# One kernel, one core: the order of work in the attention rounds changed, with the mask bias moved to VectorE

## What is computed

```python
x = x + xattn(layernorm(x), ctx, ctx, mask, gamma, beta)   # 16 x 64 queries, 1601 keys, keys are also the values
    # logits = q k^T / sqrt(512); where mask == 0: -9e15; softmax; sum over ctx; normalize; * gamma + beta
x = x + attn(layernorm(x), W_qkv, W_out)                   # softmax over the 64 rows of the own sequence
x = x + ffn(layernorm(x), router_w, expert_w1, expert_w2)  # top 2 of 8 experts, gelu, weighed by the softmax of the two
```

## Time and profile before

| what | value |
|---|---|
| median of 3 runs | 754.7 us (754.33 to 756.3) |
| the profiled execution's own time | 754.9 us |
| its span | 753.2 us |
| mean granted PE clock | 0.998 |
| PE busy | 733.2 us (97%) |
| PEld busy | 554.5 us (74%) |
| DVE busy | 435.3 us (58%) |
| ACT busy | 310.1 us (41%) |
| POOL busy | 156.3 us (21%) |
| PE in the chain that ended last | 85% of the span |
| DMA in that chain | 7% |

### The profile page before, as it was taken

How to read it: one execution, slowest core, us unless ns; L and a number is a source line. 1 busy time by engine, 2 the same in 40 slices (tenths; PEclk the granted TensorE clock), 3 DMA queues, 4 the chain that set the end, 5 groups by cost and what they waited for, 6 DMA issues and landing times.

```text
span 753.2 us, 12302 instructions
## 1 busy us (share of the span) xinstructions
PE 733.2 (97%) x4760; PEld 554.5 (74%) x4760; DVE 435.3 (58%) x980; ACT 310.1 (41%) x520; POOL 156.3 (21%) x162
## 2 busy tenths in 40 slices
PE   7899999999999999999999999999999999999996
PEld 5444354545455454578999999999999998888885
DVE  5423456666666663768975455555555565565631
ACT  2122212121212121355555556555565665656631
POOL 2132130505050401123510301310211211120201
PEclk9999999999999999999999999999999999999999
DMA  9999999999999999940645635745665656674602
GB/s 312 402 418 418 396 403 414 407 413 404 418 402 419 401 420 400 371 152 30 208 151 195 168 122 193 199 166 198 174 222 167 214 184 209 234 207 175 175 2 29
DMA packets 36477, 199.40 MB, mean 265 GB/s; under 512 B 4716, under 2 KB 5372, under 8 KB 15680
## 3 DMA queue, kind: packets, MB, share of 16 engines
q1 hardware_dynamic: 29912, 186.74, 64.5%
q0 software_dynamic: 4704, 9.14, 6.4%
q10 hardware_dynamic: 1800, 2.70, 1.1%
HBM read 188.19 MB, written 10.37 MB: 264 GB/s over the span
## 4 chain that ended last, share of the span: by engine, by line
PE 85%; DMA 7%; DVE 3%; SPq 2%; issue 1%; ACT 1%; POOL 0%; POOLq 0%
PE ps L854 11%; PE ps L813 9%; PE ps L1078 8%; PE ps L1080 8%; PE ps L1079 8%; PE ps L1100 4%; PE ps L1101 4%; PE ps L1102 4%; PE ps L1109 4%; PE ps L1110 4%; PE ps L1111 4%; PE ps L869 3%; DMA arena<-in_w_qkv 3%; DMA arena<-in_ctx 3%; PE ps L781 2%; PE ps L788 1%
## 5 line engine op out<-in xcount | busy, mean ns | idle before, releaser
L485 POOL TENSOR_TENSOR small<-small 128x1 f32<-128x1 f32 x64 | 24.4, 381 | 547.8 <-DVE yb_space L1709 196.2
L1080 PE MATMUL ps<-xT,low_a 128*128 128x288 f32 (+5 forms) x384 | 110.2, 287 | 0.0
L1291 ACT ACTIVATE hid<-ps 128x288 f32<-128x288 f32 (+5 forms) x128 | 50.6, 395 | 141.8 <-PE ps L1080 139.4
L1678 DVE TENSOR_TENSOR h_ring<-hid,h_ring 128x288 fp32r<-128x288 f32 (+5 forms) x128 | 55.6, 435 | 83.6 <-ACT h_ring L1296 83.6
L854 PE MATMUL ps<-arena 128*64 128x512 f32 (+1 forms) x416 | 95.4, 599 | 1.6 <-DMA arena<-in_ctx 0.8
L1530 DVE TENSOR_TENSOR low_a<-w_raw_a,high_b 128x2048 fp32r<-128x2048 f32 x32 | 73.3, 2291 | 37.8 <-ACT high_b L1218 37.8
L813 PE MATMUL ps<-arena 128*64 128x512 f32 x384 | 85.9, 596 | 1.1 <-DMA arena<-in_ctx_turned 0.8
L1158 ACT COPY arena<-ps 128x512 f32<-128x512 f32 (+2 forms) x90 | 42.0, 526 | 100.7 <-PE ps L788 62.8
L1078 PE MATMUL ps<-xT,high_b 128*128 128x288 f32 (+5 forms) x256 | 74.9, 293 | 0.0
L1079 PE MATMUL ps<-xT,high_b 128*128 128x288 f32 (+5 forms) x256 | 73.4, 287 | 0.0
L1080 PEld LDWEIGHTS ps<-xT,low_a 128*128 128x128 f32 x384 | 72.5, 189 | 0.0
(11 more groups left out here) (219 smaller groups left out, 1629.9 us busy)
## 6 DMA issues: line engine op xcount, KB each, us to landing
arena<-in_ctx_turned SPq DMA_DIRECT2D x48, 1024.0 KB, 22.8
arena<-in_ctx SPq DMA_DIRECT2D x48, 1024.0 KB, 18.9
w_raw_a<-in_w SPq DMA_DIRECT2D x48, 1024.0 KB, 4.9
w_raw_b<-in_w SPq DMA_DIRECT2D x16, 1024.0 KB, 4.8
arena<-in_mask SPq DMA_DIRECT2D x8, 800.5 KB, 21.4
tokens_x<-arena SPq DMA_DIRECT2D x11, 256.0 KB, 13.1
arena<-in_w_qkv SPq DMA_DIRECT2D x8, 256.0 KB, 4.7
out<-res SPq DMA_DIRECT2D x8, 256.0 KB, 9.2
```

The lines of the kernel that those rows point to most:

```text
L1080: mm = pe.matmul(o, w_low[2 * f][:, cols], high[:, k, 0:w.width], start=False, stop=(k == KC - 1))
L1291: nc.scalar.activation(hid[:, c % 2, 0:w.width], bank(c % UP_BANKS)[:, 0:w.width], ACT.Gelu).then_inc(gelu_done, 1)
L1678: dve.tensor_tensor(h_ring[:, c % RING, 1, 0:w.width], hid[:, c % 2, 0:w.width], h_ring[:, c % RING, 0, 0:w.width].bitcast(F32), ALU.subtr ...
```

## The change

The diff's parts, in the program's order. SP: the first weights for values are loaded before the first mask and the third turned block; x's tiles 3 to 7 come one by one, tile r+2 in round r. The mask bias moves from POOL to DVE (`bounds` in the DVE list: twice around `softmax(0)`, then once a round ahead of `queries`). PE: the three score blocks and the remainder stand together; `turn_second` and the router of tile r-3 come after them; `ranks` comes behind `values`; the three long `sums` stand together and `weigh` behind them. ACT's copies and DVE's routing steps follow that order. In the tail `turn_second(5)` comes ahead of the sums of tile 7 and `router(5)` behind the first of them. `fill_order` is rewritten to match.

```diff
@@ fill_order @@
-        for kind, t in (("logit", r - 3), ("xn", r - 2), ("qr", r), ("rank", r - 3), ("g", r - 2), ("s", r - 2),
-                        ("u", r - 2), ("pt", r - 2), ("out", r - 2), ("xq", r + 1), ("rest0", r + 1),
-                        ("rest1", r + 1), ("xr", r - 2)):
+        for kind, t in (("qr", r), ("xn", r - 2), ("xr", r - 3), ("g", r - 2), ("logit", r - 3), ("s", r - 2),
+                        ("u", r - 2), ("rank", r - 3), ("pt", r - 2), ("out", r - 2), ("xq", r + 1), ("rest0", r + 1),
+                        ("rest1", r + 1)):
...
@@ SP @@
             load_rest(0)
+            load_turned(0, 0)
+            load_turned(0, 1)
+            sp.dma_start(raw_v, ...).then_inc(wv_in, 16)
             load_mask(0)
-            for blk in range(NBLK - 1):
-                load_turned(0, blk)
-            sp.dma_start(raw_v, ...).then_inc(wv_in, 16)
+            load_turned(0, 2)
...
-                if r == 1:
-                    sp.dma_start(res[:, 3 * D:]..., x[3 * P:, :]...).then_inc(x_rest_in, 16)
+                if runs(r + 2):
+                    sp.dma_start(tile_of(r + 2), x[(r + 2) * P:(r + 3) * P, :]).then_inc(x_later_in[r % 2], 16)
@@ POOL: bounds() and its calls go; DVE @@
+            def bounds(j):
+                dve.wait_ge(mask_in, j * 16 + 16)
+                dve.tensor_scalar(bound, mask_sb, 0, MASKED - LIMIT, ALU.is_equal, ALU.mult).then_inc(bound_ready, 1)
@@ PE, in a round @@
                 turn_prob(r - 1)
-                if runs(r - 3):
-                    router(r - 3)
-                scores(r, 0)
-                scores(r, 1)
+                for blk in range(NBLK - 1):
+                    scores(r, blk)
+                rest_scores(r)
                 if runs(r - 2):
                     turn_first(r - 2)
-                scores(r, 2)
-                rest_scores(r)
                 if runs(r - 3):
-                    ranks(r - 3)
+                    turn_second(r - 3)
...
                     keys(r - 2)
+                if runs(r - 3):
+                    router(r - 3)
                 sums(r - 1, PV_ORDER[0])
                 if runs(r - 2):
                     own_scores(r - 2)
                     values(r - 2)
-                sums(r - 1, PV_ORDER[1])
+                if runs(r - 3):
+                    ranks(r - 3)
                 if runs(r - 2):
                     turn_own_probs(r - 2)
+                sums(r - 1, PV_ORDER[1])
                 sums(r - 1, PV_ORDER[2])
+                sums(r - 1, PV_ORDER[3])
                 if runs(r - 2):
                     weigh(r - 2)
-                sums(r - 1, PV_ORDER[3])
                 if runs(r + 1):
                     turn_query(r + 1)
                     turn_rest(r + 1)
-                if runs(r - 2):
-                    turn_second(r - 2)
 
             turn_prob(LAST)
+            turn_second(LAST - 2)
+            sums(LAST, PV_ORDER[0])
             router(LAST - 2)
-            sums(LAST, PV_ORDER[0])
             sums(LAST, PV_ORDER[1])
@@ ACT, in a round @@
+                    copy_fill("xr", r - 3, xrT, shown=by_chunk)
-                    gate_exp(r - 3)
                 exps(r)
                 if runs(r - 2):
                     copy_fill("g", r - 2, gT, shown=by_chunk)
+                if runs(r - 3):
+                    gate_exp(r - 3)
...
-                if runs(r - 2):
-                    copy_fill("xr", r - 2, xrT, shown=by_chunk)
@@ DVE @@
+            bounds(0)
             softmax(0)
+            bounds(1)
...
-                if runs(r - 3):
-                    route_first(r - 3)
-                    route_ratio(r - 3)
                 softmax(r)
                 if runs(r - 2):
                     low_xn(r - 2)
                 if runs(r - 3):
-                    gates(r - 3)
-                    route_rank(r - 3)
-                    route_second(r - 3)
+                    route_first(r - 3)
+                    route_ratio(r - 3)
                 if runs(r - 2):
                     tops(r - 2)
+                if runs(r - 3):
+                    route_rank(r - 3)
+                    gates(r - 3)
+                    route_second(r - 3)
                 if runs(r + 1):
+                    bounds(r + 1)
                     queries(r + 1)
```

More of the change, by code:

```diff
@@ L96, in fill_order @@
         yield "p", LAST, n
-    for kind, t in (("logit", LAST - 2), ("xn", LAST - 1), ("rank", LAST - 2), ("g", LAST - 1), ("s", LAST - 1),
+    for kind, t in (("xr", LAST - 2), ("logit", LAST - 2), ("xn", LAST - 1), ("rank", LAST - 2), ("g", LAST - 1), ("s", LAST - 1),
                     ("u", LAST - 1), ("pt", LAST - 1), ("xn", LAST), ("out", LAST - 1), ("g", LAST),
@@ L400, in bank @@
             return ps[:, i * BLK:(i + n) * BLK]
-        x_in, x1_in, x2_in, x_rest_in = sem("x_in"), sem("x1_in"), sem("x2_in"), sem("x_rest_in")
+        x_in, x1_in, x2_in = sem("x_in"), sem("x1_in"), sem("x2_in")
+        x_later_in = [sem(f"x_later_in{i}") for i in range(2)]
         id_in, cst_in, gb_in = sem("id_in"), sem("cst_in"), sem("gb_in")
@@ L537, in _ @@
             load_rest(0)
+            load_turned(0, 0)
+            load_turned(0, 1)
+            sp.dma_start(raw_v, w_qkv[:, 2 * WBLK:].rearrange("p (k h) -> p k h", k=KC)).then_inc(wv_in, 16)
             load_mask(0)
-            for blk in range(NBLK - 1):
-                load_turned(0, blk)
-            sp.dma_start(raw_v, w_qkv[:, 2 * WBLK:].rearrange("p (k h) -> p k h", k=KC)).then_inc(wv_in, 16)
+            load_turned(0, 2)
             sp.dma_start(raw_out, w_out.rearrange("p (k h) -> p k h", k=KC)).then_inc(wo_in, 16)
@@ L559, in _ @@
                         load_turned(r + 1, blk)
-                if r == 1:
-                    sp.dma_start(res[:, 3 * D:].rearrange("p (t d) -> p t d", d=D),
-                                 x[3 * P:, :].rearrange("(t p) d -> p t d", p=P)).then_inc(x_rest_in, 16)
+                if runs(r + 2):
+                    sp.dma_start(tile_of(r + 2), x[(r + 2) * P:(r + 3) * P, :]).then_inc(x_later_in[r % 2], 16)
                 for blk in range(NBLK - 1):
@@ L617, in _ @@
             own = Steps(pool, p_own)
[L619 to L625, removed]
             def add_bias(j):
@@ L654, in _ @@
                 pool.memset(small[:, 24 + n:25 + n], 0.0).then_inc(places_free, 1)
-            bounds(0)
             pool.wait_ge(gb_in, 32)
             add_bias(0)
-            bounds(1)
             pool.wait_ge(zero_out, 16)
@@ L661, in _ @@
                 add_bias(r)
-                if runs(r + 1):
-                    bounds(r + 1)
                 if runs(r - 3):
@@ L1261, in _ @@
                     copy_rest(r + 1)
-                if runs(r - 2):
-                    copy_fill("xr", r - 2, xrT, shown=by_chunk)
             copy_probs(LAST)
+            copy_fill("xr", LAST - 2, xrT, shown=by_chunk)
             gate_exp(LAST - 2)
@@ L1384, in queries @@
             def queries(p):
-                dve.wait_ge((x_in, x1_in, x2_in, x_rest_in)[min(p, 3)], 16)
+                if p < 3:
+                    dve.wait_ge((x_in, x1_in, x2_in)[p], 16)
+                else:
+                    dve.wait_ge(x_later_in[p % 2], (p - 1) // 2 * 16)
                 if p >= 1:
@@ L1416, in attended @@
                 if j == 0:
+                    dve.wait_ge(gb_in, 32)
                     dve.wait_ge(filled, filled_at("vo", 0, KC - 1))
```

## The result

The changed kernel takes 760.7 us (median of 6 executions, 759.9 to 761.7) beside 755.2 for the kernel before in the same session (753.8 to 756.3): the ratio is 1.0073 [1.0063, 1.0084]. It is slower by 5.5 us, more than the 0.3% that can be told from no change, and it lies above the range of the prediction (753.3 to 759.3). The profiled execution has 760.06 us of its own time and a span of 758.3, 5.1 over the span before. Its mean granted clock of PE is 0.991 (0.998 before).

What follows compares the result with a forecast made beforehand. Loads set the pace up to 114.56 us, PE after that, DVE joining at the end of round 7. -4.2 + 5.0 + 0.9 = +1.7 on 754.9 gave 756.6 profiled, 756.4 us median; range 753.3 to 759.3.

Steps and rivals of the forecast that it cites:

- The step that failed: Tail: from tile 7's first sums PE runs gapless to `keys(6)`, only the router's 0.9 us added, all behind follows.
- the tail's waits: Tail: `weigh(5)` ends last, DVE's 7.5 us follow nearly uncovered; tile 7's sums start 0.85 us later, 5.0 of the gain gone.
- the router: Tail: tile 5's router, formerly done while PE waited for DVE, now stands among tile 7's sums: 0.9 us more.
- The gain ahead of the tail: Up to T (end of `rest_scores`) of round 7: 2.4 us by round 3 plus 4 x 0.45, 4.2 us gained.
- Breaks between 64 and 128 columns: PE, each round: six stretches of 64-column work become three, 0.29 us per break pair, 0.87 us a round saved.
- The two short waits: PE, each round: `keys` waits 0.24 us for ACT's copy, `turn_prob` 0.2 for its banks; together bounded by 0 and 0.8.
- Wait (b): Ahead of `turn_prob`: its banks must be freed by copies of `weigh`'s result and of the query; 0.2 us a round.
- Rival (1): Slower: waits at `keys` and `turn_prob` cost their upper bound, 0.4 us more a round; 758.6 us; chance 0.25.
- rival (2): Waits at `keys` and `turn_prob` cost nothing, 5 x 0.44 us less; 754.4 us; chance 0.15.
- before 92: Sign of being wrong: round 2's third score block starting before 92 us; forecast 92.7, set by its turned context landing.
- Rival (3): Faster: the 1.6 us gained at the start pass through if round 2's turned context lands earlier; up to 752.8; chance 0.12.
- rival (4): DVE late inside rounds: late mask or longer stretch holds the query, `copy_pt` and `weigh`; 761 us; chance 0.03.

Runs made afterwards that it cites:

- experiment 1: Changed kernel plus products nobody reads (20 ahead of tile 5's second turn, 24 ahead of tile 7's first sums); 757.5 us, 1.0031 of the kernel before.
- experiment 6: Kernel of experiment 5 with `weigh` ahead of the last long sums in every round, not only round 7; 755.03 us, 0.9995 of the kernel before.
- experiment 9: Kernel of experiment 5 with the first loads in their old order (values' weights behind mask and third turned block); 753.42 us, 0.9979 of the kernel before.
- experiment 11: Kernel of experiment 10 plus products nobody reads in PE's waits (34 ahead of tile 5's second turn, 7 ahead of tile 7's sums); 758.05 us, 1.0047.
- experiment 10: Kernel before the change with `weigh(5)` moved behind the last long sums, in round 7 alone; 761.14 us, 1.0076 of the kernel before.
- experiment 8: Kernel of experiment 5 with x's tiles 3 to 7 in one load again, in round 1; 755.78 us, 1.0006 of the kernel before.
- experiment 7: Kernel of experiment 5 with the mask bias back on POOL; 754.31 us, 0.9984 of the kernel before.
- kernel 4: Changed kernel with `weigh` ahead of the last sums in round 7 alone and tile 5's router back ahead of tile 7's first sums; 753.98 us, 0.9981.
- kernel 12: Kernel of experiment 5 with 9 more products nobody reads, in short waits before the experts begin; 752.58 us, 0.9965 of the kernel before.
- experiment 5: Kernel 4 plus products nobody reads: 7 ahead of tile 5's router, 3 ahead of tile 7's first sums; 753.25 us, 0.9977 of the kernel before.

## Why the prediction was wrong

**The step that failed** is the sentence "From there on PE runs without a gap up to `keys(6)`", used to set everything behind tile 7's first sums to its old length. There is no gap, but PE runs at the lower of its two clocks there, because of the waits just ahead of it. The sum had the tail's waits (+5.0, measured +5.2) and the router (+0.9, measured +1.1), and lacked a term for the clock: 3.1 us by the rows, 3.2 by experiment 1. With it 756.4 becomes 759.5. The gain ahead of the tail was sized too high as well, 4.2 for 3.3, and with that and the two small differences the sum comes to 760.8, where 760.7 was measured. None of the rivals carried the clock, so the range was too narrow as well. The Trainium skill, "TensorE: Matmul & The Clock Gate", HAM oscillation, names the mechanism: it describes a kernel whose short bursts of products alternate with waits for loads and restart at the lower clock each time. Here the trace shows the same once, behind shorter waits and for DVE, with a granted clock of 0.50 for the restart.

**Breaks between 64 and 128 columns:** right. 0.29 for a pair, and 0.30 measured (experiment 6). The Trainium skill, "TensorEngine Tiling (Array Packing)", Key Properties, with the fixed part from "TensorE: Matmul & The Clock Gate", Single matmul latency, gave an estimate of 0.33 for the pair; the trace is nearer to the rows' price, though the two are too close for the runs to rule the other out.

**The two short waits:** right in place, a little small. The round is 36.13, not 36.0. `keys` takes 3.84 instead of 3.67 behind its wait, a part of the upper bound that I had named. Wait (b) comes from the query's copy alone: with `weigh` further ahead it stayed (experiment 6). Of what was saved per round, 0.32 is left of the 0.45. Rival (1) needed a round of 36.3 or more, and rival (2) one without waits: both fall. (Their 758.6 and 754.4 were counted from the 756.6 of the profiled execution, 0.2 more than the median's sum.)

**The start:** right that nothing is gained by the earlier weights (experiment 9). Round 2's block came at 91.35 and not at 92.72, but that is no effect of the order: over the fourteen traces of this study it starts anywhere between 90.9 and 93.2, in the old order too (90.9 and 91.1 in experiments 11 and 10), and what follows shifts with it. So "before 92", named as a sign of being wrong, could not tell the order's effect from this spread. Of the 4.6 us at T of round 7, 1.4 is luck of that execution, and that T came out at 275.1 beside the forecast 275.5 is luck too: behind the block 3.3 us were gained and not 4.2. Rival (3) falls. **From the block to round 3** 2.4 us were predicted and 2.0 found; the split load of x is what gave them, 1.8 by the traces and 2.2 by the medians (experiment 8).

**DVE inside the round:** hidden, as said; rival (4) falls (experiment 7). My 1.82 for the mask instruction was far too high. The Trainium skill's "VectorE: DVE Perf Modes", The perf-mode tier table, by which I had estimated 1.0, is borne out with 0.99.

**The chances:** slower had 0.44 and no change 0.48. The named rival for slower was a wait in the rounds, not the tail. The place of the loss was in the forecast itself, with 5.9 us for it, and half as much again was missing.

**What stays open:** how the waits of some 0.4 us at the handover are followed by a lower clock in some executions and not in others, of these kernels and perhaps of the kernel before (mean clock 0.992 to 0.999 in its timed runs), and why 0.74 us in the tail of kernel 4 were, and 0.77 in the kernel before not. Fillers ended it in the six executions of kernel 12; a longer series was not run. And of the 3.1 us between the medians of experiments 10 and 11 the rows of the tail explain 0.5.

## What to carry to other kernels

When an order is regrouped so that a dependent step comes last in each round, look at the last round by itself: there the next round's work, which hid the step's consumer, is gone, and one call in one of seven rounds cost 5 us where all the rounds had saved less than 2. Price a wait of TensorE twice, by its length and by the clock of what follows it: here waits of 2.25 and 2.78 us cost 3.1 more, in products that nothing else held up; in experiment 10 the slow products lay beside DVE's work and cost 0.5. Count gains from a point that the first loads no longer move, or luck of one execution passes for a hit. Where such a wait can't be removed, a few idle transposes into a free bank are a cheap cover, and a version with the regrouping, the step moved in the last round only and such fillers took 0.9965 of the time before.

## What the runs showed of the hardware

- A wait of only 0.74 us, with a few idle tenths before and behind it, was followed by a fallen clock too: 4.51 us of sums took 6.21 (experiment 4). In the kernel before, waits of 0.26 and 0.77 us in the same stretch were not.
- Transposes of a constant tile held the granted clock at 1.00 through stretches in which PE had nothing else to do (experiments 1, 5, 11 and 12).
- A VectorE tensor_tensor of 128 x 512 from float32 takes 0.68 us in the changed kernel and 2.16 on average where the mask instruction over 1,601 elements is on POOL (experiment 7); in the round of the earlier trace rows it took 2.94, all of it beside POOL's 5.63. It cost nothing in either kernel, since DVE had that time.
- An instruction from int32 to float32 over 1,601 elements, an odd number, took 0.99 us on VectorE.
- The turned context of round 2, loaded through full DMA engines, let PE go on at 90.9 us in one execution and at 93.2 in another, and all that follows up to `keys(6)` shifts with it: a likely source of the kernels' spread, besides the clock.
